# Scores from scaled 16-bit planes of keys and queries, in a two-layer cross-attention and feed-forward kernel

## What is computed

```python
q = (query @ wq).reshape(bs, sq, 32, 128).transpose((0, 2, 1, 3))
k = (key @ wk).reshape(bs, sk, 8, 1, 128)      # each of 8 key heads serves 4 query heads
...
q = _apply_rope(q, curr_seq_pos)
k = _apply_rope(k, curr_seq_pos)
raw = jnp.einsum('bhqd,bhkd->bhqk', q, k) / scale
# + mask, softmax over k, product with v, product with wo
```

## Time and profile before

| | |
|---|---|
| median of 3 runs | 2069.71 us (2067.95 to 2070.38) |
| the profiled execution | 2063.38 us |
| its span, first to last instruction | 2061.6 us |
| busy: TensorE, VectorE, ScalarE, GpSimd | 2001.8, 1599.0, 1080.4, 1266.2 us |
| granted TensorE clock, mean | 0.992 |

### The profile page before, as it was taken

How to read it: one execution, slowest core, us unless ns; L and a number is a source line. 1 busy time by engine, 2 the same in 40 slices (tenths; PEclk the granted TensorE clock), 3 DMA queues, 4 the chain that set the end, 5 groups by cost and what they waited for, 6 DMA issues and landing times.

```text
span 2061.6 us, 26211 instructions
## 1 busy us (share of the span) xinstructions
PE 2001.8 (97%) x9118; PEld 1235.3 (60%) x9122; DVE 1599.0 (78%) x2903; ACT 1080.4 (52%) x1674; POOL 1266.2 (61%) x751
## 2 busy tenths in 40 slices
PE   8999999999889999999999999999999999999899
PEld 6877786877645555555555555555555555555487
DVE  5776776676678888888888888888888888888743
ACT  3443353336466566565655656566565656656400
POOL 1552352422167788887778877777777778875500
PEclk9999999999999999999999999999999999999999
DMA  7663675455998787887778899887787887877612
GB/s 267 225 208 118 210 242 174 164 178 170 311 214 175 160 172 146 182 174 164 169 159 172 174 217 215 214 172 174 153 174 166 165 188 144 168 161 144 193 62 72
DMA packets 673379, 366.32 MB, mean 178 GB/s; under 512 B 576768, under 2 KB 593408, under 8 KB 671200
## 3 DMA queue, kind: packets, MB, share of 16 engines
q1 hardware_dynamic: 673248, 364.65, 72.1%
HBM read 182.12 MB, written 39.85 MB: 108 GB/s over the span
## 4 chain that ended last, share of the span: by engine, by line
PE 77%; DVE 6%; DMA 3%; issue 2%; ACT 2%; POOL 2%; SPq 0%; ACTq 0%; DVEq 0%; POOLq 0%
PE ps L43 25%; PE ps L45 24%; PE ps L44 24%; PE ps L876 1%; POOL u_sb L2134 1%; DMA pT<-pp 1%; DVE t_sb L1239 1%; DMA raw<-in_ctx 1%; DVE pp L1658 1%; DVE psb L1641 0%; DVE vhl_sb L1311 0%; ACT wh L1797 0%; DVE u_sb L1239 0%; PE ps L1133 0%; PE ps L883 0%
## 5 line engine op out<-in xcount | busy, mean ns | idle before, releaser
L2175 POOL TENSOR_SCALAR araw<-araw,sc 128x512 f32<-128x512 f32 x256 | 563.2, 2200 | 51.9 <-DMA araw<-in_wq 51.9
L1658 DVE SCALAR_TENSOR_TENSOR pp<-psb,st,pp 128x1024 f16<-128x1024 f32 x256 | 400.3, 1564 | 3.5 <-ACT pp L2027 1.5
L2020 ACT ACTIVATE psb<-psb,st 128x1024 f32<-128x1024 f32 x256 | 294.7, 1151 | 195.7 <-DVE st L1644 195.7
L2027 ACT ACTIVATE pp<-psb,st 128x1024 f16<-128x1024 f32 x256 | 294.4, 1150 | 159.7 <-DVE st L1653 154.5
L1641 DVE CUSTOM_DVE_ANT_0 psb<-ps,mask 128x1024 f32<-128x1024 f32 x256 | 313.4, 1224 | 70.4 <-PE ps L45 67.5
L43 PE MATMUL ps<-ksb,qsb 128*128 128x512 f32 x512 | 250.8, 490 | 9.5 <-DVE st L1641 6.9
L2181 POOL TENSOR_TENSOR wol<-araw,woh 128x512 f16<-128x512 f32 x128 | 149.0, 1165 | 109.4 <-ACT woh L1953 109.4
L43 PE MATMUL ps<-woh,osb 128*128 128x512 f16 x512 | 195.0, 381 | 9.2 <-issue 4.8
L45 PE MATMUL ps<-ksb,qsb 128*128 128x512 f32 x512 | 203.0, 396 | 0.0
L44 PE MATMUL ps<-ksb,qsb 128*128 128x512 f32 x512 | 202.6, 396 | 0.0
L1674 DVE SCALAR_TENSOR_TENSOR x_lo<-ps,sc,x_lo 128x512 f32<-128x512 f32 x256 | 190.4, 744 | 14.0 <-PE ps L45 12.8
(11 more groups left out here) (283 smaller groups left out, 3981.4 us busy)
## 6 DMA issues: line engine op xcount, KB each, us to landing
araw<-in_wq SPq DMA_DIRECT2D x128, 256.0 KB, 4.7
araw<-in_wo SPq DMA_DIRECT2D x128, 256.0 KB, 4.3
k_scratch<-khl SPq DMA_DIRECT2D x32, 512.0 KB, 3.6
scan<-in_wq SPq DMA_DIRECT2D x64, 256.0 KB, 4.9
scan<-in_wo SPq DMA_DIRECT2D x64, 256.0 KB, 4.7
ksb<-k_scratch SPq DMA_DIRECT2D x16, 1024.0 KB, 6.1
raw<-in_wv SPq DMA_DIRECT2D x16, 512.0 KB, 5.0
raw<-in_ctxT SPq DMA_DIRECT2D x16, 512.0 KB, 4.5
```

The costliest lines, as they stand in the source:

```text
L1658: e.scalar_tensor_tensor(out=pp[:, r, 1024:2048], in0=psb[:, r, :], scalar=st[:, n // 4 % 4, 16 + i:17 + i], in1=pp[:, r, 0:1024], op0=ALU ...
L2020: e.activation(P, P, ACT.Exp, bias=c[:, 4 + i:5 + i], accum_out=c[:, 8 + i:9 + i]).then_inc(a_exp.sem, 1)
L2027: e.activation(pp[:, r, 0:1024], psb[:, r, :], ACT.Copy, scale=st[:, n // 4 % 4, 16 + i:17 + i]).then_inc(a_ph.sem, 1)
L2175: e.tensor_scalar(w_raw(n), w_raw(n), sc[:, 16 + wo:17 + wo], None, ALU.mult).then_inc(p_ws.sem, 1)
```

## The change

Keys and rotated queries become 16-bit planes, as the other operands of layer 1 are. For that they are scaled by powers of two. The bound for a key head comes from the squares of the context and of that head's key weights: ScalarE makes 24 squares of 128x1024 (`key_square`: 16 context tiles, 8 key weight tiles), TensorE sums them over partitions in 9 small 32-bit matmuls (`key_squares`), VectorE makes the scale in 5 small dependent operations each (`key_scale`). The key's rotation applies it (`scaled_rope`). The scale of the queries now goes into the query weights (`scale_w`), so the two operations on the tables are gone. The scores come out multiplied by a known factor: the exponent's scale and the negated maximum take it back with a scalar read from memory, and the mask is multiplied by its inverse, 4 tiles a batch (`scale_mask`). Key planes in memory and in transfers have half the bytes.

```diff
-    k_d = nc.dram_tensor("k_scratch", [16, 128, 2, 1024], F32, kind="Internal").ap()
+    k_d = nc.dram_tensor("k_scratch", [16, 128, 2, 1024], F16, kind="Internal").ap()
...
-    khl = alloc(one, "khl", [128, 2, 2, 512], F32R)
+    khl = alloc(one, "khl", [128, 2, 2, 512], F16)
...
-    ksb = alloc(two, "ksb", [128, 2, 2, 1024], F32R)
+    ksb = alloc(two, "ksb", [128, 2, 2, 1024], F16)
...
-    qsb = alloc(two, "qsb", [128, 2, 2, 512], F32R)
+    qsb = alloc(two, "qsb", [128, 2, 2, 512], F16)
...
+    KEY_SUM_AT = {0: 0, 5: 1, 9: 2, 13: 3, 17: 4, 20: 5, 25: 6, 29: 7, 32: "c1"}
...
+        def key_squares(key):
+            ...
+            if key in (0, "c1"):
+                e.wait_ge(v_cq.sem, v_cq[1 if key else 0])
+            if key != "c1":
+                e.wait_ge(a_kq.sem, a_kq[key])
+            a, z = (1, 3) if key == 0 else (0, 1) if key == "c1" else (2 + key, 3 + key)
+            e.matmul(ps[:, 7 if key == 5 else 4, a:z], twos[:, :], ksq[:, 16 + a:16 + z], start=True, stop=True).then_inc(
+                t_kc.sem, 1)
...
             kv_products(group)
+            if s in KEY_SUM_AT:
+                key_squares(KEY_SUM_AT[s])
...
+        def scaled_rope(src, scale, cos, sin, u, t):
+            e.scalar_tensor_tensor(out=u, in0=src, scalar=scale, in1=cos, op0=ALU.mult, op1=ALU.mult)
...
+        def context_squares(b):
+            e.wait_ge(a_kq.sem, a_kq["c", 8 * b + 7])
+            e.tensor_reduce(ksq[:, 17 - b:18 - b], ksq[:, 8 * b:8 * b + 8], AX, ALU.add).then_inc(v_cq.sem, 1)
...
+        def key_scale(key):
+            ...
+            e.wait_ge(t_kc.sem, t_kc[key])
+            e.tensor_scalar(kst[:, a:z], ps[:, 7 if key == 5 else 4, a:z], 2.0 ** -60, 2.0 ** 60, ALU.max,
+                            ALU.min).then_inc(v_kc.sem, 1)
+            ...
...
                 split_lo("w2" if s == 0 else "w18")
+                context_squares(s // 32)
                 kv_end(s)
                 kv_end(s + 1)
+                key_scale(KEY_SUM_AT[s])
                 kv_end(s + 2)
...
+        def key_square(key):
+            ...
+            e.wait_ge(a_hi.sem, a_hi[name])
+            if key != ("c", 0):
+                e.wait_ge(a_kq.sem, a_kq[key] - 1)
+            e.activation(junk[:, :], f32(split_dst(name, 0)), ACT.Square, accum_out=ksq[:, at:at + 1]).then_inc(a_kq.sem, 1)
...
         for key in SPLIT_ORDER[:10]:
             split_hi(key)
+            if key in ("c5", "c6", "c7"):
+                key_square(("c", int(key[1:]) - 5))
+        for c in range(3, 8):
+            key_square(("c", c))
+        key_square(0)
...
+            floor_roots(2, "w", 3)
+            e.tensor_scalar(sc[:, 16:17], sc[:, 12:13], sc[:, 13:14], 2.0 ** 14, ALU.mult, ALU.mult).then_inc(v_ws.sem, 1)
+            ...
+            e.tensor_scalar(kst[:, 30:38], kst[:, 12:20], sc[:, 16:17], None, ALU.mult).then_inc(v_ws.sem, 1)
+            ...
+            e.tensor_scalar(sc[:, 22:24], kst[:, 10:12], sc[:, 18:19], None, ALU.mult).then_inc(v_ws.sem, 1)
+            ...
+            e.reciprocal(kst[:, 38:40], sc[:, 22:24]).then_inc(v_ws.sem, 1)
...
-                e.tensor_scalar(cosq[:, :], cosq[:, :], sc[:, 18:19], None, ALU.mult).then_inc(v_ws.sem, 1)
-                e.tensor_scalar(sinq[:, :], sinq[:, :], sc[:, 18:19], None, ALU.mult).then_inc(v_ws.sem, 1)
...
+        def scale_mask(b, i):
+            e.wait_ge(d_m[i].sem, d_m[i][b])
+            e.tensor_scalar(mask[:, i, :], mask[:, i, :], kst[:, 39 - b:40 - b], LOWEST, ALU.mult, ALU.max).then_inc(v_m.sem, 1)
...
-            e.tensor_scalar(c[:, 4 + i:5 + i], c[:, i:i + 1], -1.0, None, ALU.mult).then_inc(v_nmax.sem, 1)
+            e.tensor_scalar(c[:, 4 + i:5 + i], c[:, i:i + 1], sc[:, 23 - H // 32:24 - H // 32], -1.0, ALU.mult,
+                            ALU.mult).then_inc(v_nmax.sem, 1)
...
-            e.activation(P, P, ACT.Exp, bias=c[:, 4 + i:5 + i], accum_out=c[:, 8 + i:9 + i]).then_inc(a_exp.sem, 1)
+            e.activation(P, P, ACT.Exp, bias=c[:, 4 + i:5 + i], scale=sc[:, 23 - H // 32:24 - H // 32], accum_out=c[:, 8 + i:9 + i]).then_inc(a_exp.sem, 1)
...
-                e.tensor_scalar(w_raw(n), w_raw(n), sc[:, 16 + wo:17 + wo], None, ALU.mult).then_inc(p_ws.sem, 1)
+                G = W_ORDER[n][1] // 8 % 8
+                scale = sc[:, 17:18] if wo else kst[:, 30 + G:31 + G]
+                e.tensor_scalar(w_raw(n), w_raw(n), scale, None, ALU.mult).then_inc(p_ws.sem, 1)
```

More of the change, by code:

```diff
@@ L174, in build_in @@
     staged.close()
-    khl = alloc(one, "khl", [128, 2, 2, 512], F32R)
+    khl = alloc(one, "khl", [128, 2, 2, 512], F16)
+    junk = alloc(one, "junk", [128, 1024], BF16)
+    alloc(one, "junk_pad", [128, 1024], F16)
     ctab = alloc(one, "ctab", [128, 1024])
@@ L407, in build_in @@
     t_htr = signal("t_htr", [("f", i) for i in range(8)] + h_tiles)
+    t_kc = signal("t_kc", [*range(8), "c1"])
     t_rt = signal("t_rt", ["w", 0, 1, "v"])
@@ L423, in build_in @@
     v_kr = signal("v_kr", KS)
+    v_kc = signal("v_kc", [(key, j) for key in [*range(8), "c1"] for j in range(5)])
+    v_cq = signal("v_cq", range(2))
+    v_m = signal("v_m", [(b, i) for b in range(2) for i in range(4)])
     v_sc = signal("v_sc", [(G, j) for G in range(16) for j in range(7)])
@@ L434, in build_in @@
     v_h2 = signal("v_h2", range(8))
-    v_ws = signal("v_ws", [("w", j) for j in range(7)] + [("v", j) for j in range(2)] + ["cosq", "sinq"]
-                  + [("v", j) for j in range(2, 12)])
+    v_ws = signal("v_ws", [("w", j) for j in range(11)] + [("v", j) for j in range(12)])
     v_rt = signal("v_rt", [(b, j) for b in range(2) for j in range(8)])
@@ L458, in build_in @@
     a_vh = signal("a_vh", VS)
+    a_kq = signal("a_kq", [("c", c) for c in range(8)] + [*range(8)] + [("c", c) for c in range(8, 16)])
     a_khi = signal("a_khi", KS + [(i, j) for i in range(8) for j in range(2)])
@@ L1794, in split_hi @@
                 e.wait_ge(t_kv.sem, t_kv[2 * (n - 2) + 1])
+            if key[0] == "w" and n % 2 and 1 < n < 18:
+                e.wait_ge(a_kq.sem, a_kq[(n - 3) // 2])
             if key[0] == "c" and n > 8:
+                e.wait_ge(a_kq.sem, a_kq["c", n - 9])
                 e.wait_ge(t_kv.sem, t_kv[(31, n - 9) if n < 16 else 31 if n == 16 else (63, n - 17)])
@@ L1884, in scalar_program @@
                     split_hi(f"c{c}")
+                    key_square(("c", c - 2))
+                for c in (14, 15):
+                    key_square(("c", c))
             if len(group) > 1:
@@ L1900, in scalar_program @@
                 split_hi(f"w{s // 2 + 2}")
+                if s < 29 and s % 4 == 3:
+                    key_square(s // 4 + 1)
             if s in A_TURN_AT:
```

88 lines of the change are left out of this document (70 added, 18 removed).

## The result

The changed kernel takes 2076.01 us (median of 6 runs, 2071.39 to 2079.21) beside 2067.44 us for the kernel before (6 runs, 2062.48 to 2070.38): ratio 1.0042, 95% interval 1.0024 to 1.006. It is slower by 0.4%; the prediction was 0.5% faster, and its range (2047 to 2066) does not hold the time. The profiled execution took 2071.39 us with a span of 2069.6, against 2063.38 and 2061.6 before.

A forecast was written before the change was run, and what follows sets the result against it. TensorE was taken to bound attention, with neighbours close behind. Attention -20.5, its start -0.5 and the part ahead +9.8 made -11.2 us, so 2058.5 us, 0.5% faster; own range 2050 to 2065, whole range 2047 to 2066.

The forecast's parts named there:

- The scores: Attention's score matmuls: 16-bit planes remove 0.108 us from each of 256 groups, laid to weight loads; -27.6 us.
- the rival in which it came with the start of a group: Score groups: the 0.108 stays because loads were hidden anyway, costs remain; slower, 2080 us, chance 0.07.
- Even heads: `wo_part(p, 0)` in attention: 18 heads already waiting for `o_lo` lose 0.11 + 0.10 each; +3.9 us.
- `pT`: Start of `values` in attention: some heads wait for the last transpose; +2.5 us, ends 0 and 10.
- The mask of batch 1: Ahead of head 32's first maxima: four scalings on VectorE, mostly in idle time; +0.7 us.
- The exponent: Attention loop: reading its scale from memory is free, as it is bound by its 1024 elements.
- Ahead of attention: Whole first stage and query scaling before attention: +9.8 us, ends 5 and 15.
- The start: Start of the kernel: seven squares delay `w2`, TensorE waits 3.9 us and its clock falls; +5.7, ends 2.5 and 7.
- The eight small matmuls: First stage: those after the first group cost TensorE 0.25 us each; 2.0 us.
- The group at step 32: First stage: squares stand between casts TensorE already waits for; +1.2 us, ends 0.5 and 4.
- the chains take over: Attention: max, exponent, planes and transpose set each head, so the gain halves; 2066 us, chance 0.11.
- the margin for `pT`: Before `values`: 0.6 us of slack behind the last transpose, falling by 0.34; most heads keep some.

The follow-up runs named there:

- run 3: Kernel before with only the 16-bit planes of keys and queries, unscaled, and none of the scaling work: 2041.35 us, ratio 0.9877.
- run 5: Changed kernel with VectorE's two small row_scale operations moved ahead of `p_lo` at w = 0: 2049.96 us, ratio 0.9912.
- run 4: Changed kernel with constants, not scalars from memory, for exponent and negated maximum, giving other probabilities: 2067.33 us, ratio 0.9996.
- run 7: Kernel before with unscaled 16-bit planes of keys and queries, and `q_hi` moved behind `o_hi` on ScalarE: 2027.27 us, ratio 0.981.
- run 1: Changed kernel with `q_hi` moved from ahead of `o_hi` to right behind it on ScalarE: 2056.82 us, ratio 0.9951.
- run 2: Kernel before with `q_hi` moved behind `o_hi` on ScalarE: 2057.78 us, ratio 0.9956.
- run 6: Changed kernel with the first stage's squares and small matmuls put at other places, none left out: 2072.13 us, ratio 1.003.
- run 8: Changed kernel with the edits of run 1, run 5 and run 6, and batch 1's mask scaled before the wait for scores: 2047.25 us, ratio 0.9901.

## Why the prediction was wrong

**The scores (-27.6): the size right, the cause open.** Loads of 98 ns, steps across a score group of 1.51 us, and with the chain away heads of 20.72 to 20.85 for 21.15: the 0.10 a group went with the type, so the rival in which it came with the start of a group falls. That the weight load was the cause is not shown. Keys (the weights) and queries (what streams past them) changed their type together, and the 0.10 lay on all 32-bit steps alike (0.232 us for 0.216); the 24 matmuls of a step of the first stage, on 32-bit planes in both kernels, take 5.44 us, 0.227 each. The Trainium skill ("TensorE: Matmul & The Clock Gate", Step-by-step: what each phase is for) has the engine pull a weight load ahead of matmuls in flight. Whether the loads of 191 ns were hidden that way and the queries cost the time, or the loads did, no run here tells.

**Even heads (+3.9): this step failed.** The prediction saw the chain and its wait, and took "18 x (0.11 + 0.10)": the stall grows by one score group and one longer negated maximum. (The product is 3.8, and with the 0.12 worked out in the sentence before it would be 4.1.) It grew by 0.50, from 0.34 to 0.84, and stood in 23 heads of 52 and not in 18: some 13 us. Two things were overlooked. First, the chain does not start with the scores but with VectorE. In the turns ahead of `values` TensorE's turn is 18 matmuls, 3.88 us, and VectorE's work in it is `p_lo`, row scale 0.30, `wo_add` 0.74, maximum 1.22 and its readings 0.3. VectorE before the change:

```profile
1414.82 1.23 DVE L1641 CUSTOM_DVE_ANT_0 psb<-ps,mask 128x1024 f32<-128x1024 f32 x1 [0.26 <-PE ps L45]
...
1416.16 1.76 DVE L1658 SCALAR_TENSOR_TENSOR pp<-psb,st,pp 128x1024 f16<-128x1024 f32 x1
```

and after it, without a wait from 1398.16 on:

```profile
1402.07 1.21 DVE L1728 CUSTOM_DVE_ANT_0 psb<-ps,mask 128x1024 f32<-128x1024 f32 x1
...
1403.45 2.05 DVE L1746 SCALAR_TENSOR_TENSOR pp<-psb,st,pp 128x1024 f16<-128x1024 f32 x1
...
1406.34 1.22 DVE L1728 CUSTOM_DVE_ANT_0 psb<-ps,mask 128x1024 f32<-128x1024 f32 x1
```

Before, VectorE's last turn (from maximum to maximum) took 3.99 us, as long as TensorE's with one 32-bit group in it. Now TensorE's takes 3.88 and VectorE's 4.27, as `p_lo` has grown from 1.77 to 2.05 us (means of 26 heads; GpSimd works beside it, and with constants, in run 3, it is as long). So the last maximum of the head started 0.19 us after `values` before and starts 0.59 after it now (1406.34 after 1405.75), and GpSimd's sum begins 4.11 us after `values` and not 3.73. This 0.38 together with the 0.11 of the earlier `wo_part` is the 0.50. Some 0.1 of the 0.38 is TensorE's shorter turn, the rest VectorE's longer one; why `p_lo` grew is not shown. So the head lost not the gain of "the one score group inside that stretch", 0.11, but more than that of all four, 0.43. Second, the 2.36 us of the sum was taken as its price. It is one of two outcomes of a race, and 1.26 is the other; which one comes decides 0.8 us of a head.

**`pT` (+2.5): too small, inside its ends.** The wait at the start of `values` grew by 6.3 us between 700 and 1880 us.

**The mask of batch 1 (+0.7): right only where the chain has slack.** The three heads from 31 on cost 3.4 us more after the change and 1.1 less with the planes alone, so 4.5; in run 5 they cost 0.1 more than before. The operations last 0.74 to 1.15 us each. They stand behind the wait for the scores on an engine that was late already.

**The exponent, called free.** It went from 1151 to 1241 ns and the negated maximum from 154 to 214; 3 to 9 us (run 4). The four terms, 13, 6, 4.5 and the 3 of run 4's trace, overlap a little, but together they are the 27.5 us that attention lost again.

**Ahead of attention (+9.8): the sum was near (+6.5), two terms were not.** The start: forecast 5.7, measured 4.4 at steps 4 and 5; the wait was 2.4 us and not 3.9, as the seven squares, 1.24 each, began at 24.61 and not at 25.61 (the last context tile came earlier in this trace), and `w2` was cast at 33.12 and not at 34.4. The granted clock behind it was 0.57 from 36 to 40 us. (The wait ahead of 156 us, from which the price of the clock was taken, is 2.6 us in the trace and not 3.0.) The eight small matmuls cost 0.25 each where they did not wait, as forecast. The group at step 32: 2.4 for 1.2. Missing were the stall at key 5 (5.9, of which 3.8 came back), and on the other side the 8 to 11 us that halved key planes save in this stage (runs 3 and 7). The scaling costs 14 to 17 us there (the changed kernel and run 1 against runs 3 and 7), not 10. The error was to take little but the first group as late: each small matmul is a place where TensorE can wait for the queue of ScalarE, and of the other eight only the one at step 32 was given a wait.

**The rivals.** What happened is "the chains take over", given 0.11 and 2066. In kind it was right, as shorter steps turned to waits behind a chain from the maximum; but the chain was another than the one it names (rotation, sum, `q_hi` and `o_lo`, not exponent, planes and transpose), and half of the gain was to stay where none did. Its test, the margin for `pT`, pointed at the wrong wait: that margin did go in most heads (the median from landing to `values` fell from 0.73 to 0.25 us), but it cost 6 us; the margin that mattered was that of `o_lo`, which was below zero already in 18 heads.

## What to carry to other kernels

A saving on the engine that is busiest is worth only what the next engine's turn leaves of it: before forecasting it, add up the neighbour's work in the shortest turn, and look for a wait that is above zero already, since the saving upstream of it can be lost there. Where two engines start within a tenth of a microsecond, look at both durations over all rounds; a minimum and a median a factor of two apart can be a race, and the order that settles it can be worth more than the change (26 us here, for two small operations moved). Price a change of type and the scaling that it needs apart: here, with the exchange on ScalarE, they were -30 and +30.

## What the hardware showed that was not expected

VectorE's `p_lo` (three operands of 128x1024 in SBUF, one of them written) and GpSimd's sum of two 128x512 tiles do not run beside one another. Started 0.05 us apart, VectorE first, one takes its own time and the other nearly the sum of both: 1.28 and 2.36, or 2.39 and 1.26. Neither has a fixed priority: with the same order of the two instructions the sum lost in 18 of 26 odd heads before the change, 23 after it, and in 13 to 26 of 26 in the traces of runs 1 to 4, 6 and 7. With a lead of 0.2 us (runs 5 and 8) it won in all. What tips it in a close start was not found.

An activation with its scale from memory takes 1241 ns where one with a constant takes 1151, for 128x1024 elements; a `tensor_scalar` of one column 214 for 154.

Steps of matmuls with 512 columns are 0.216 us apart on 16-bit planes and 0.227 to 0.232 on 32-bit ones, at the full clock in both.
